# One attention loop of a twelve-stage kernel: maxima over one and two PSUM banks in turn, half sums by a product with a 0/1 matrix, value products in two bursts

## Chip, cores and metric

One core of a Trainium2 chip. The metric is the device time of one execution of the whole program in microseconds (us), the median of the runs shown.

## What is computed

The reference is a chain of four layers, each half a mixture of experts, an attention, half a mixture again, on x of shape (2, 1024, 128) in float32. The change lies in the attention of the first layer. With 16 heads of 8 channels, two batches and 1024 tokens it is a full softmax attention:

```
qp = (q @ wq.T + bq) * dh ** (-0.5); kp = k @ wk.T + bk; vp = v @ wv.T + bv
s = jnp.einsum('bqhd,bkhd->bhqk', qh, kh)
a = jax.nn.softmax(s, axis=-1)
o = jnp.einsum('bhqk,bkhd->bqhd', a, vh).reshape(B, Lq, D)
return o @ w_out.T + b_out
```

(There is a small attention across the two batches beside it, done once ahead of the loop.)

## The kernel before

Everything is written out by hand: five engines, each with its own list of instructions, and semaphores between them. The class `Full` and its functions `full_sync`, `full_pool`, `full_tensor`, `full_scalar` and `full_vector` are the first attention. Loops over the 32 pairs of a head and a batch are called phases here; four phases make a `turn` (`SLOTS` = 4), the first and the last turn stand alone and the six between them are a hardware loop.

q and k are split into three bf16 parts each and stored to DRAM; for a phase SyncE loads them back into one of four slots of `stack`, 72 rows of products, so that one bf16 product of 128 columns of stationary against 512 of moving gives a tile of exact scores (`by_query`, L1734: queries on the partitions, and `by_key`, L1751: keys on the partitions).

The softmax needs the maximum of each query before the exponential. So a phase does two things at once, for different heads and batches:

- for the phase two ahead, the maxima: 16 products `by_query` (8 query tiles of two halves of 512 keys), each reduced by VectorE to one number a partition (`piece`, L1947) into `nm2`. Products go through a ring of three banks, 0 to 2 (`RING`, `item`): product number i may be made when VectorE has done with number i - 3 (`ring_free`). When the 16 are done, `both_halves` (L1955) joins the halves, TensorE transposes the 8 columns (`turn_max`, L1742, an item of the ring too), VectorE copies them out (`max_out`, L1964), GpSimd splits them into three bf16 parts (`max_parts`, L1661 to L1664) and SyncE writes them as three more rows into the slot (`max_rows`, L1606), in time for the `by_key` of the next phase, which then gives scores minus maximum.
- for its own head and batch, scores by key: eight times two products into two banks (3 and 4 or 5 and 6), the exponential by ScalarE over both (L1877) into `pT`, and value products.

The value products (`values`, L1766) are f32, with 9 stationary columns (8 channels and a column of ones, which gives the softmax's sum) and 512 moving columns. Four of them run side by side in four column tiles of the array, all into bank 7: two halves of the queries, times odd and even key tiles. There are four such bursts of four products in a phase (m = 0 to 3), after the key tiles 4, 6 and 7 and, for m = 3, in the second step of the next phase. Since they all accumulate, a bf16 product of zeros clears the bank first (L1761).

Then bank 7 is copied by ScalarE (`o_copy`, L1864), transposed back by TensorE in four transposes into bank 7 (`by_token`, L1774), and VectorE adds the odd and the even half (`sums`, L1970) and takes the reciprocal of the sums (L1974); GpSimd divides (`divide`, L1669).

The order on TensorE within a phase, for kt = 0 to 7: a `by_query`, the two products of `by_key(kt)`, a `by_query`; after kt = 1 `turn_max` and the last value burst of the phase before; after kt = 2 `by_token` of the phase before; after kt = 4, 6 and 7 a value burst. Ahead of the loop stand two rounds of 16 maxima alone (the prologue), and the last two phases have none.

Of the kernel before, what the change touches and what calls it, by code (L numbers as in the profile page):

```python
# [8 lines left out]
ALU = mybir.AluOpType  # L9
# [3 lines left out]
P = 128  # L13
D = 128
B = 2
# [1481 lines left out]
class Full:  # L1497
# [17 lines left out]
    RING, SLOTS, PHASES = 3, 4, HEADS * B  # L1515
    TURNS = PHASES // SLOTS
    MAXIMA = TB * QH
    STEP = MAXIMA + 1
    LOADS, MAX_LOADS = 2 * 3 + 1, 3

    def __init__(self, k, n, w):
# [22 lines left out]
        self.oT_used = k.sem(f"{n}_oT_used")  # L1544
# [12 lines left out]
        self.nm2 = nm2.rearrange("p (a t h) -> p a t h", a=2, h=self.QH)  # L1557
# [13 lines left out]
    def item(self, t, q, i, alone=False):  # L1571

        at = (4 if not alone else 0) if i is None else i + (i >= 4 and q != -2)
# [55 lines left out]
def full_pool(pool, k, s):  # L1631
# [41 lines left out]
    def turn(t, first=False, last=False):  # L1673
        for q in range(s.SLOTS):
            n = t * s.SLOTS + q
            begin = first and q == 0
            fixed_values(n, t * (s.SLOTS // B) + q // B, q % B, q % 2, first=first and q < 2)
            if not (last and q == s.SLOTS - 1):
                if q == 0 and not first:
                    pool.wait_ge(s.stacked[s.SLOTS - 1], t * lap)  # L1680
                if q:
                    pool.wait_ge(s.stacked[q - 1], t * lap + lap)
                max_parts(n + 1, s.item(t, q, None, last and q == s.SLOTS - 2)[0], (q + 1) % 2)
            if not begin:
                divide(n - 1, t * (s.SLOTS // B) + (q - 1) // B, (q - 1) % B)

    max_parts(0, s.item(None, -1, None)[0], 0)
# [9 lines left out]
def full_tensor(pe, k, s):  # L1697
# [28 lines left out]
    def by_query(t, q, i, slot, laps):  # L1726

        _, bank, free = s.item(t, q, i)
        qt, half = divmod(i, s.QH)
        if i == 0:  # L1730
# [3 lines left out]
        pe.matmul(k.ps[:, bank, :], s.stack[:, slot, 0, qt * P:(qt + 1) * P],  # L1734
                  s.stack[:, slot, 1, half * GW:(half + 1) * GW], start=True, stop=True).then_inc(s.ring_full, 1)

    def turn_max(t, q, n, alone=False):

        _, bank, free = s.item(t, q, None, alone)
        pe.wait_ge(s.negmax, n + 1)  # L1740
        pe.wait_ge(s.ring_free, free)
        pe.transpose(k.ps[0:TB, bank, 0:P], s.nm, k.ident[:, :]).then_inc(s.ring_full, 1)  # L1742
# [12 lines left out]
    def values(n, m, place, first=False):  # L1755

        if m == 0:
            pe.wait_ge(s.vg, n + 1)
            if not first:
                pe.wait_ge(s.oT_used, n)  # L1760
            pe.matmul(k.ps[:, 7, :], k.zeros[:, 0:P], k.zeros[:, :], start=True, stop=False, skip_group_check=True)  # L1761
        pe.wait_ge(s.probs, n * TB + (2 * m + 2))
        for h in range(s.QH):
            for odd in range(2):
                at = 32 * (2 * h + odd)
                ins = pe.matmul(k.ps[at:at + s.DH + 1, 7, :], s.vs[:, place, 2 * m + odd, :],  # L1766
                                s.pT[:, 2 * m + odd, h * GW:(h + 1) * GW], start=False, stop=(m == TB // 2 - 1),
                                tile_position=(0, at), skip_group_check=True)
        ins.then_inc(s.values, 1)

    def by_token(n):
        pe.wait_ge(s.o_out, n + 1)
        for j in range(GT):
            ins = pe.transpose(k.ps[:, 7, j * P:(j + 1) * P], s.o[:, j * P:(j + 1) * P], k.ident[:, :])  # L1774
        ins.then_inc(s.oT_mm, 1)

    def turn(t, first=False, last=False):
        for q in range(s.SLOTS):
            n = t * s.SLOTS + q
            begin = first and q == 0  # L1780
            more = not (last and q >= s.SLOTS - 2)
            for kt in range(TB):
                if more:
                    by_query(t, q, 2 * kt, (q + 2) % s.SLOTS, t + (1 if q >= 2 else 0))
                by_key(n, kt, q, t, begin)
                if more:
                    by_query(t, q, 2 * kt + 1, (q + 2) % s.SLOTS, t + (1 if q >= 2 else 0))
# [9 lines left out]
    for i in range(s.MAXIMA):  # L1797
        by_query(None, -2, i, 0, 0)
    for i in range(s.MAXIMA):
        by_query(None, -1, i, 1, 0)  # L1800
        if i == 3:
            turn_max(None, -1, 0)
# [3 lines left out]
    turn(s.TURNS - 1, last=True)  # L1806
    values(s.PHASES - 1, 3, 1)
# [23 lines left out]
def full_scalar(act, k, s):  # L1831
# [51 lines left out]
    o_copy(s.PHASES - 1)  # L1883
    for g in range(NG):
# [5 lines left out]
def full_vector(dve, st, k, s):  # L1890
# [51 lines left out]
    def piece(t, q, i, place):  # L1942

        number, bank, _ = s.item(t, q, i)
        qt, half = divmod(i, s.QH)
        dve.wait_ge(s.ring_full, number + 1)
        dve.tensor_reduce(s.nm2[:, place, qt, half:half + 1], k.ps[:, bank, :], AX.X, ALU.max, negate=True)\  # L1947
            .then_inc(s.ring_free, 1)

    def both_halves(done, turned, place):  # L1950
# [4 lines left out]
        dve.tensor_reduce(s.nm, s.nm2[:, place, :, :], AX.X, ALU.min).then_inc(s.negmax, 1)  # L1955

    def max_out(t, q, n, alone=False):

        number, bank, _ = s.item(t, q, None, alone)
        dve.wait_ge(s.ring_full, number + 1)  # L1960
# [3 lines left out]
        dve.tensor_copy(s.nmf[0:TB, :], k.ps[0:TB, bank, 0:P]).then_inc(s.ring_free, 1)  # L1964

    def sums(n, first=False):
        dve.wait_ge(s.oT_mm, n + 1)
        if not first:
            dve.wait_ge(s.normalized, n)
        dve.tensor_reduce(s.sums[:, :, :].rearrange("p (h j) e -> p j h e", h=s.QH),  # L1970
                          k.ps[:, 7, :].rearrange("p (j h o z) -> p j h z o", j=GT, h=s.QH, o=2)[:, :, :, 0:s.DH + 1, :],
                          AX.X, ALU.add).then_inc(s.oT_used, 1)
        dve.wait_ge(s.oT_used, n + 1)
        dve.reciprocal(s.rsum[:, :], s.sums[:, :, s.DH]).then_inc(s.divisor, 1)  # L1974

    def turn(t, first=False, last=False):
        for q in range(s.SLOTS):
# [3 lines left out]
            if not (last and q == s.SLOTS - 1):  # L1981
                start, _, _ = s.item(t, q, 0)

                both_halves(start, start - 12, (q + 1) % 2)
            for kt in range(TB):
                if kt == 3 and not begin:
                    sums(n - 1, first=first and q == 1)
                if more:
                    piece(t, q, 2 * kt, q % 2)
                    piece(t, q, 2 * kt + 1, q % 2)  # L1990
# [3 lines left out]
    for i in range(s.MAXIMA):  # L1994
        piece(None, -2, i, 0)
    both_halves(s.MAXIMA, None, 0)
    for i in range(s.MAXIMA):
        piece(None, -1, i, 1)
        if i == 3:
            max_out(None, -1, 0)  # L2000
# [4 lines left out]
    sums(s.PHASES - 1)  # L2005
# [43 lines left out]
def build(nc, ins, out, plan):  # L2049
    with ExitStack() as ctx:  # L2050
# [24 lines left out]
        A0.wg, A0.wl, A0.cols = k.sb("l0a_wg", [P, 4, P]), k.sb("l0a_wl", [P, 4, P]), k.sb("l0a_cols", [P, 10])  # L2075
        A0.block, A0.bo, A0.blo, A0.scaled = k.sb("l0a_block", [P, P]), k.sb("l0a_bo", [P, D]), k.sb("l0a_blo", [1, D]), k.sb("l0a_scaled", [P, 2])
# [31 lines left out]
        def loads():  # L2108
# [9 lines left out]
            for m, dst in (("wg", A0.wg), ("wl", A0.wl), ("cols", A0.cols), ("block", A0.block), ("blo", A0.blo)):  # L2118
# [134 lines left out]
def layout(a):  # L2253
# [73 lines left out]
    out["l0a_block"] = out["l3_block"]  # L2327
    out["l0a_bo"], out["l0a_blo"] = a["L0_attn_bg_out"][None], a["L0_attn_bl_out"][None]
# [23 lines left out]
```

## Time and profile before

| | us |
|---|---|
| median of 3 runs | 2480.91 (2479.04 to 2482.99) |
| profiled execution | 2483.68 |
| its span, first to last instruction | 2481.9 |
| mean granted TensorE clock | 0.941 |

How to read the profile: times are microseconds from the start of the span; PE is TensorE's products, PEld its weight loads, DVE VectorE, ACT ScalarE, POOL GpSimd, SP SyncE. A group of instructions is named by line, engine, operation, out<-in and count; behind it stand the idle time of the engine just before it and what ended that. An f32 product appears as two records (two passes). Products are pipelined: a 512-column bf16 product is shown with 0.38 us but the next one starts 0.215 us later, so busy time of PE runs over short gaps, and an idle time of PEld is no idle time of the array. A few product records are missing.

### The profile page before, as it was taken

To read this page: it belongs to the slowest core of one execution; us is meant where nothing else is said; L and a number is where in the kernel's file an instruction comes from. 1 tells how busy PE (TensorE), PEld (TensorE's weight loads), DVE (VectorE), ACT (ScalarE), POOL (GpSimd) and SP (SyncE) were. 2 spreads that over 40 slices of the span, in tenths; PEclk is the share of its full clock that TensorE was granted. 3 is DMA by queue.
4 is the path that set the end of the run, shared out by engine and by line. 5 is a ranking of instruction groups with operands and counts; after the bars stand their busy time and mean duration, and the time that the engine had idled before them with its cause. 6 is when DMAs were issued, how large, how long until landed. Compare 5 with 4: busy or idle time off the path is not lost.

```text
span 2481.9 us, 39071 instructions
## 1 busy us (share of the span) xinstructions
PE 2165.2 (87%) x13425; PEld 1352.2 (54%) x13466; DVE 1570.0 (63%) x4488; ACT 1034.4 (42%) x1761; POOL 155.9 (6%) x273
## 2 busy tenths in 40 slices
PE   4559999995699989898999887999999579998698
PEld 3413333334577755555555554677766357775476
DVE  7688989858543346666665665334446735687766
ACT  2116767672143434444444443433333233343133
POOL 5111111114000000000000000000000000000000
PEclk8669999997799999999999999999999789999899
DMA  5020000000000000000000000000010000000000
GB/s 211 1 74 27 26 25 25 25 11 1 1 1 1 1 1 1 1 0 0 0 0 0 0 1 1 1 1 1 3 52 1 0 1 1 1 1 1 1 1 18
DMA packets 20864, 32.05 MB, mean 13 GB/s; under 512 B 5657, under 2 KB 12194, under 8 KB 19970
## 3 DMA queue, kind: packets, MB, share of 16 engines
q1 hardware_dynamic: 20738, 30.40, 3.6%
q8 instruction: 76, 1.25, 0.2%
q14 instruction: 50, 0.41, 0.1%
HBM read 25.80 MB, written 4.19 MB: 12 GB/s over the span
## 4 chain that ended last, share of the span: by engine, by line
PE 62%; DVE 10%; issue 3%; ACT 3%; DVEq 0%; ACTq 0%; POOL 0%; POOLq 0%
PE ps L404 18%; PE ps L389 18%; PE ps L600 6%; PE ps L634 5%; PE ps L617 4%; PE ps L584 3%; DVE arena L796 1%; ACT arena L730 1%; DVE x L814 1%; PE ps L606 1%; PE ps L330 1%; PE ps L252 1%; PE ps L896 1%; DVE stat L129 1%; PE ps L1050 1%
## 5 line engine op out<-in xcount | busy, mean ns | idle before, releaser
L404 PEld LDWEIGHTS ps<-l_w,arena 128*128 128x128 f32 x4096 | 543.6, 194 | 262.1 <-issue 248.4
L404 PE MATMUL ps<-l_w,arena 128*128 128x128 f32 x4096 | 546.8, 277 | 12.7 <-DVE x L491 10.9
L389 PE MATMUL ps<-xnT,l_w 128*128 128x512 f32 x1024 | 536.4, 607 | 3.0 <-ACT xnT L260 3.0
L491 DVE SCALAR_TENSOR_TENSOR x<-ps,comb,x 128x128 f32<-128x128 f32 x768 | 216.2, 344 | 378.2 <-PE ps L404 376.4
L447 ACT ACTIVATE arena<-ps,l_b 128x512 f32<-128x512 f32 x384 | 263.7, 687 | 408.9 <-PE ps L389 408.7
L1947 DVE TENSOR_REDUCE arena<-ps 128x1 f32<-128x512 f32 x512 | 325.5, 684 | 38.0 <-PE ps L1734 35.9
L1877 ACT ACTIVATE arena<-ps 128x1024 f32<-128x1024 f32 x256 | 252.5, 1023 | 128.6 <-PE ps L1751 128.2
L730 ACT ACTIVATE arena<-ps,arena 128x128 f32<-128x128 f32 (+7 forms) x256 | 187.1, 744 | 168.8 <-DVE arena L796 168.8
L796 DVE TENSOR_REDUCE arena<-ps 128x1 f32<-128x128 f32 (+7 forms) x256 | 179.0, 751 | 98.6 <-PE ps L606 98.6
L1734 PE MATMUL ps<-arena 128*128 128x512 bf16 x480 | 174.9, 398 | 6.7 <-DMA arena<-s_parts_k 4.1
L600 PE MATMUL ps<-arena 64*128 64x512 f32 (+3 forms) x768 | 151.1, 512 | 19.7 <-ACT arena L730 18.2
L389 PEld LDWEIGHTS ps<-xnT,l_w 128*128 128x128 f32 x1024 | 159.0, 195 | 16.5 <-issue 11.8
L617 PE MATMUL ps<-ident,arena 128*128 128x128 f32 x1152 | 163.8, 278 | 4.6 <-ACT arena L738 3.8
L803 DVE COPY arena<-ps 128x512 f32<-128x512 f32 (+1 forms) x192 | 99.0, 550 | 101.5 <-PE ps L617 99.4
L617 PEld LDWEIGHTS ps<-ident,arena 128*128 128x128 f32 x1152 | 128.1, 141 | 51.9 <-issue 27.7
L1751 PE MATMUL ps<-arena 128*128 128x512 bf16 x503 | 151.0, 382 | 4.0 <-DVE arena L1947 2.5
L738 ACT ACTIVATE arena<-ps 128x512 f32<-128x512 f32 (+1 forms) x192 | 86.1, 489 | 153.7 <-PE ps L617 153.4
L483 DVE SCALAR_TENSOR_TENSOR x<-l_b,comb,x 128x128 f32<-128x128 f32 x512 | 145.8, 347 | 4.2
L1734 PEld LDWEIGHTS ps<-arena 128*128 128x128 bf16 x512 | 50.2, 98 | 168.3 <-DVE arena L1947 122.1
L447 ACT ACTIVATE arena<-ps 128x512 f32<-128x512 f32 x128 | 76.5, 597 | 148.0 <-PE ps L389 147.7
L634 PE MATMUL ps<-arena 128*64 128x256 f32 (+3 forms) x1152 | 134.9, 383 | 0.9 <-issue 0.9
L1766 PE MATMUL ps<-arena,xn 128*9 128x512 f32 x1024 | 133.9, 595 | 0.1
(318 smaller groups left out, 2057.3 us busy)
## 6 DMA issues: line engine op xcount, KB each, us to landing
arena<-s_parts_q SPq DMA_DIRECT2D x96, 48.0 KB
arena<-s_parts_k SPq DMA_DIRECT2D x96, 48.0 KB
l_w<-in_l_w SPq DMA_DIRECT2D x2, 2048.0 KB, 14.2
l_w<-in_l_w SPq DMA_DIRECT2D x4, 1024.0 KB, 12.6
s_parts_q<-arena SPq DMA_DIRECT2D x2, 768.0 KB, 4.2
s_parts_k<-arena SPq DMA_DIRECT2D x2, 768.0 KB, 4.9
arena<-arena SPq DMA_DIRECT2D x96, 2.0 KB
x<-in_x SPq DMA_DIRECT2D x4, 256.0 KB, 3.5
```

The source lines that it names most:

```text
L389: pe.matmul(k.ps[:, n % 2, :], w.w1[:, e, f * P:(f + 1) * P], k.xnT[:, g * GW:(g + 1) * GW], start=True, stop=True).then_inc(s.hidden_mm.s ...
L404: ins = pe.matmul(k.ps[:, 2 + e % 4, j * P:(j + 1) * P], w.h[:, n % 2, j * P:(j + 1) * P], w.w2[:, e, f, :], start=(f == 0 and j == 0), st ...
L447: act.activation(w.h[:, n % 2, :], k.ps[:, n % 2, :], s.func, **kw).then_inc(s.hidden.sem, 1)
L491: ins = dve.scalar_tensor_tensor(k.x[:, t, :], k.ps[:, 2 + e % 4, j * P:(j + 1) * P], k.comb[:, t, e:e + 1], k.x[:, t, :], ALU.mult, ALU.add)
L600: pe.matmul(k.ps[:, 2 * h + i + c // GW, 0:n], s.q[rows, b, qt * P:(qt + 1) * P], s.kT[rows, b, c:c + n], start=True, stop=c + n < width, ...
L617: ins = pe.transpose(k.ps[:, 4 + i, j * P:(j + 1) * P], s.p[:, 2 * (u % 2) + h, at + j * P:at + (j + 1) * P], k.ident[:, :])
L634: ins = pe.matmul(k.ps[64 * h:64 * h + 64, 6, at:hi], s.v[:, b * TB + kt, 64 * h:64 * h + 64], s.pT[:, h, kt, at:hi], start=(kt == 0), sto ...
L730: ins = act.activation(s.p[:, 2 * (u % 2) + h, at:at + width], src[:, at:at + width], ACT.Exp, bias=s.nm[:, u % 2, h, i:i + 1], accum_out= ...
L796: ins = dve.tensor_reduce(s.nm[:, u % 2, h, i:i + 1], src[:, at:at + width], AX.X, ALU.max, negate=True)
L1734: pe.matmul(k.ps[:, bank, :], s.stack[:, slot, 0, qt * P:(qt + 1) * P], s.stack[:, slot, 1, half * GW:(half + 1) * GW], start=True, stop=T ...
L1877: act.activation(s.pT[:, kt, :], k.ps[:, bank:bank + 2, :].rearrange("p a b -> p (a b)"), ACT.Exp)\
L1947: dve.tensor_reduce(s.nm2[:, place, qt, half:half + 1], k.ps[:, bank, :], AX.X, ALU.max, negate=True)\
```

## The change

- The maxima of a phase are made in 11 groups, six of one product (always bank 2) and five of two products (banks 0 and 1), in turn, with the transpose of the maxima (bank 0) as the fourth of 12 places. One reduce of VectorE covers a group. A group may be made when the group two places back has been reduced. The order on TensorE is a table, `GROUPS_AT[kt, place]`, place 0 ahead of `by_key(kt)`, place 1 behind it.
- The clearing product is done once, in the first phase; each column tile's first value product starts its sum itself (`start=(m == 0)`).
- Value products come in two bursts of two steps: m = 0 and 1 after kt = 6, m = 2 and 3 after kt = 1 of the next phase.
- Four f32 products with the columns of `o` as the stationary operand and a 0/1 matrix `sel` (128 x 18, loaded with the weights) as the moving one take the place of the four transposes; they add odd and even halves. ScalarE copies the 72 numbers a partition to `sums` after the fourth exponential of the next phase, and VectorE only takes the reciprocal, ahead of its groups of kt = 4.

```
-    RING, SLOTS, PHASES = 3, 4, HEADS * B
+    SLOTS, PHASES = 4, HEADS * B
+    TURNED = 3
+    GROUPS = [(0, 1), (1, 3), (3, 4), None, (4, 5), (5, 7), (7, 8), (8, 10), (10, 11), (11, 13), (13, 14), (14, 16)]
+    STEP = len(GROUPS)
+    GROUPS_AT = {(0, 0): 0, (0, 1): 1, (1, 0): 2, (2, 0): 4, (2, 1): 5, (3, 0): 6, (3, 1): 7, (4, 0): 8, (5, 0): 9,
+                 (6, 0): 10, (7, 1): 11}
...
+    def group(self, t, q, j, alone=False):
+
         if t is None:
-            number = at + (self.MAXIMA if q == -1 else 0)
-            return number, number % self.RING, number - self.RING + 1
-        place = self.STEP * q + at
-        number = t * (self.STEP * self.SLOTS) + (self.MAXIMA + self.STEP + place)
-
-        return number, place % self.RING, number - (1 if place < 2 else self.RING - 1)
+            number = j - (q == -2 and j > self.TURNED) + (q == -1) * (self.STEP - 1)
+            return number, number - (0 if q == -2 and j == self.TURNED + 1 else 1)
+        number = 2 * self.STEP - 1 + (t * self.SLOTS + q) * self.STEP + (0 if alone else j)
+        return number, number - (0 if alone else 1)
...
+    def maxima(t, q, j, slot, laps):
+
+        _, free = s.group(t, q, j)
+        if j == 0:
             pe.wait_ge(s.stacked[slot], laps * lap + 16 * s.LOADS)
         if not (t is None and free <= 0):
             pe.wait_ge(s.ring_free, free)
+        lo, hi = s.GROUPS[j]
+        for i in range(lo, hi):
+            qt, half = divmod(i, s.QH)
+            ins = pe.matmul(k.ps[:, 2 if hi - lo == 1 else i - lo, :], s.stack[:, slot, 0, qt * P:(qt + 1) * P],
+                            s.stack[:, slot, 1, half * GW:(half + 1) * GW], start=True, stop=True)
+        ins.then_inc(s.ring_full, 1)
...
         if m == 0:
             pe.wait_ge(s.vg, n + 1)
-            if not first:
-                pe.wait_ge(s.oT_used, n)
-            pe.matmul(k.ps[:, 7, :], k.zeros[:, 0:P], k.zeros[:, :], start=True, stop=False, skip_group_check=True)
+            if first:
+                pe.matmul(k.ps[:, 7, :], k.zeros[:, 0:P], k.zeros[:, :], start=True, stop=True)
+            else:
+                pe.wait_ge(s.sums_out, n)
...
-            ins = pe.transpose(k.ps[:, 7, j * P:(j + 1) * P], s.o[:, j * P:(j + 1) * P], k.ident[:, :])
+            ins = pe.matmul(k.ps[:, 7, j * 18:(j + 1) * 18], s.o[:, j * P:(j + 1) * P], w.sel[:, :],
+                            start=True, stop=True)
...
+                for place in range(2):
+                    if more and (kt, place) in s.GROUPS_AT:
+                        maxima(t, q, s.GROUPS_AT[kt, place], (q + 2) % s.SLOTS, t + (1 if q >= 2 else 0))
+                    if place == 0:
+                        by_key(n, kt, q, t, begin)
                 if kt == 1 and not (last and q == s.SLOTS - 1):
                     turn_max(t, q, n + 1, alone=not more)
                 if kt == 1 and not begin:
+                    values(n - 1, 2, (q - 1) % 2)
                     values(n - 1, 3, (q - 1) % 2)
                 if kt == 2 and not begin:
                     by_token(n - 1)
-                if kt in (4, 6, 7):
-                    values(n, (4, 6, 7).index(kt), q % 2, first=begin)
+                if kt == 6:
+                    values(n, 0, q % 2, first=begin)
+                    values(n, 1, q % 2)
...
+    def sums(n, first=False):
+        act.wait_ge(s.oT_mm, n + 1)
+        if not first:
+            act.wait_ge(s.normalized, n)
+        act.activation(s.sums[:, :, :].rearrange("p (h j) e -> p j h e", h=s.QH),
+                       k.ps[:, 7, 0:18 * GT].rearrange("p (j h e) -> p j h e", h=s.QH, e=s.DH + 1), ACT.Copy)\
+            .then_inc(s.sums_out, 1)
...
+    def maxima(t, q, j, place):
+
+        lo, hi = s.GROUPS[j]
+        dve.wait_ge(s.ring_full, s.group(t, q, j)[0] + 1)
+        dve.tensor_reduce(s.nm2[:, place, lo:hi], k.ps[:, 2:3, :] if hi - lo == 1 else k.ps[:, 0:2, :],
+                          AX.X, ALU.max, negate=True).then_inc(s.ring_free, 1)
```

## Rows read from the trace of the kernel before

**Rows 1.** The page: span, and busy time, share and instructions of each engine.
```profile
span 2481.9 us, 39071 instructions
PE 2165.2 (87%) x13425; PEld 1352.2 (54%) x13466; DVE 1570.0 (63%) x4488; ACT 1034.4 (42%) x1761; POOL 155.9 (6%) x273
```

**Rows 2.** Windows, steady loop: length, busy PE PEld DVE ACT POOL, PEclk, DMA, GB/s.
```profile
300.00:420.00 120.00, 118.95 (x684) 38.12 (x696) 107.62 (x199) 83.94 (x90) 22.07 (x60) 1.00 0.08 26
```

**Rows 3.** Waits, 303 to 400 us: waiting <- releaser: us, times, longest.
```profile
PEld ps L1734 <- DVE arena L1947: 31.2, 41, 0.9
ACT arena L1877 <- PE ps L1751: 27.1, 40, 1.1
DVE arena L1947 <- PE ps L1734: 8.8, 30, 0.4
```

**Rows 4.** Line L1955 (once in each phase), same stretch: ns min/median/max, first and last start.
```profile
L1955 DVE TENSOR_REDUCE arena<-arena x8: 169/170/171, 315.0 to 399.9; 128x8 f32<-128x16 f32 x8
```

**Rows 5.** Groups of instructions, same stretch: count, busy us, mean ns, idle before.
```profile
L1947 DVE TENSOR_REDUCE arena<-ps 128x1 f32<-128x512 f32 x128 | 81.6, 685 | 9.2 <-PE ps L1734 8.8 <-remote 0.4
L1877 ACT ACTIVATE arena<-ps 128x1024 f32<-128x1024 f32 x64 | 63.1, 1023 | 27.1 <-PE ps L1751 27.1
...
L1970 DVE TENSOR_REDUCE arena<-ps 128x72 f32<-128x144 f32 x8 | 2.4, 297 | 0.0
```

**Rows 6.** Timeline, a phase's first part: start us, us, instruction, count, idle before.
```profile
400.24 0.59 PE L1751 MATMUL ps<-arena 128*128 128x512 bf16 x2
...
401.10 0.59 PE L1751 MATMUL ps<-arena 128*128 128x512 bf16 x2
...
401.83 0.27 PE L1742 MATMUL ps<-ident,arena 128*8 128x128 f32 x1
...
402.03 1.04 PE L1766 MATMUL ps<-arena,xn 128*9 128x512 f32 x8
...
403.01 0.39 PE L1734 MATMUL ps<-arena 128*128 128x512 bf16 x1
...
403.15 0.60 ACT L1864 ACTIVATE xn<-ps 128x512 f32<-128x512 f32 x1 [0.26 <-PE ps L1766]
...
403.44 0.69 DVE L1947 TENSOR_REDUCE arena<-ps 128x1 f32<-128x512 f32 x1 [0.28 <-PE ps L1734]
```

**Rows 7.** Timeline, the next 2.5 us: the transposes, a reduce and its follower.
```profile
403.89 0.60 PE L1774 MATMUL ps<-ident,xn 128*128 128x128 f32 x4
...
405.15 0.67 DVE L1947 TENSOR_REDUCE arena<-ps 128x1 f32<-128x512 f32 x1
...
405.87 0.39 PE L1734 MATMUL ps<-arena 128*128 128x512 bf16 x1
```

**Rows 8.** Timeline in a mixture: f32 products, 128x128 stationary, 8 columns.
```profile
674.68 3.27 PE L330 MATMUL ps<-l_gate,xnT 128*128 128x8 f32 x28
```

**Rows 9.** Timeline, second round of the prologue and start of phase 0.
```profile
157.87 2.00 PE L1734 MATMUL ps<-arena 128*128 128x512 bf16 x4 [2.59 <-DMA arena<-s_parts_k]
...
165.20 2.07 SPq L1606 DMA_DIRECT2D arena<-arena  x3
...
168.48 1.03 PE L1751 MATMUL ps<-arena 128*128 128x512 bf16 x2
```

**Rows 10.** Timeline: by_key starts of phases 30 and 31, first transpose after the loop.
```profile
533.59 1.04 PE L1751 MATMUL ps<-arena 128*128 128x512 bf16 x4
...
542.95 1.04 PE L1751 MATMUL ps<-arena 128*128 128x512 bf16 x4
...
556.00 1.35 PE L1813 MATMUL ps<-ident,acc 128*128 128x128 f32 x6 [1.08 <-POOL acc L1669]
```

**Rows 11.** Windows of later stages, columns as in Rows 2.
```profile
900.00:960.00 60.00, 48.40 (x319) 29.95 (x318) 32.57 (x75) 27.09 (x70) 0.53 (x2) 0.93 0.00 1
960.00:1240.00 280.00, 252.22 (x1882) 161.00 (x1882) 176.54 (x364) 136.42 (x342) 2.79 (x10) 1.00 0.00 0
1240.00:1560.00 320.00, 276.21 (x2047) 176.13 (x2044) 197.22 (x443) 147.67 (x361) 2.49 (x9) 0.98 0.00 0
```

More of the change, by code:

```diff
@@ L1569, in __init__, with start @@
         self.v = k.xnT.rearrange("p (t d) -> p t d", d=P)
-    def item(self, t, q, i, alone=False):
-        at = (4 if not alone else 0) if i is None else i + (i >= 4 and q != -2)
+    def group(self, t, q, j, alone=False):
         if t is None:
-            number = at + (self.MAXIMA if q == -1 else 0)
-            return number, number % self.RING, number - self.RING + 1
-        place = self.STEP * q + at
-        number = t * (self.STEP * self.SLOTS) + (self.MAXIMA + self.STEP + place)
-        return number, place % self.RING, number - (1 if place < 2 else self.RING - 1)
+            number = j - (q == -2 and j > self.TURNED) + (q == -1) * (self.STEP - 1)
+            return number, number - (0 if q == -2 and j == self.TURNED + 1 else 1)
+        number = 2 * self.STEP - 1 + (t * self.SLOTS + q) * self.STEP + (0 if alone else j)
+        return number, number - (0 if alone else 1)
+    def start(self, t, q):
+        return 2 * self.STEP - 1 + (t * self.SLOTS + q) * self.STEP
 def full_sync(sp, k, s):
@@ L1682, in turn @@
                     pool.wait_ge(s.stacked[q - 1], t * lap + lap)
-                max_parts(n + 1, s.item(t, q, None, last and q == s.SLOTS - 2)[0], (q + 1) % 2)
+                max_parts(n + 1, s.group(t, q, s.TURNED, last and q == s.SLOTS - 2)[0], (q + 1) % 2)
             if not begin:
                 divide(n - 1, t * (s.SLOTS // B) + (q - 1) // B, (q - 1) % B)
-    max_parts(0, s.item(None, -1, None)[0], 0)
+    max_parts(0, s.group(None, -1, s.TURNED)[0], 0)
     turn(0, first=True)
@@ L1733, in by_query @@
             pe.wait_ge(s.ring_free, free)
-        pe.matmul(k.ps[:, bank, :], s.stack[:, slot, 0, qt * P:(qt + 1) * P],
-                  s.stack[:, slot, 1, half * GW:(half + 1) * GW], start=True, stop=True).then_inc(s.ring_full, 1)
+        lo, hi = s.GROUPS[j]
[4 more added lines that the diff above has]
+        ins.then_inc(s.ring_full, 1)
     def turn_max(t, q, n, alone=False):
-        _, bank, free = s.item(t, q, None, alone)
+        _, free = s.group(t, q, s.TURNED, alone)
         pe.wait_ge(s.negmax, n + 1)
         pe.wait_ge(s.ring_free, free)
-        pe.transpose(k.ps[0:TB, bank, 0:P], s.nm, k.ident[:, :]).then_inc(s.ring_full, 1)
+        pe.transpose(k.ps[0:TB, 0, 0:P], s.nm, k.ident[:, :]).then_inc(s.ring_full, 1)
     def by_key(n, kt, slot, laps, first):
@@ L1766, in values @@
                 ins = pe.matmul(k.ps[at:at + s.DH + 1, 7, :], s.vs[:, place, 2 * m + odd, :],
-                                s.pT[:, 2 * m + odd, h * GW:(h + 1) * GW], start=False, stop=(m == TB // 2 - 1),
+                                s.pT[:, 2 * m + odd, h * GW:(h + 1) * GW], start=(m == 0), stop=(m == TB // 2 - 1),
                                 tile_position=(0, at), skip_group_check=True)
@@ L1793, in turn @@
                     by_token(n - 1)
-                if kt in (4, 6, 7):
-                    values(n, (4, 6, 7).index(kt), q % 2, first=begin)
[L1797 to L1802, printed above, removed]
+                if kt == 6:
+                    values(n, 0, q % 2, first=begin)
+                    values(n, 1, q % 2)
+    for q in (-2, -1):
+        for j in range(s.STEP):
+            if j != s.TURNED:
+                maxima(None, q, j, q + 2, 0)
+            elif q == -1:
+                turn_max(None, q, 0)
     turn(0, first=True)
@@ L1806, in full_tensor @@
     turn(s.TURNS - 1, last=True)
+    values(s.PHASES - 1, 2, 1)
     values(s.PHASES - 1, 3, 1)
@@ L1872, in turn @@
                     o_copy(n - 1, first=first and q == 1)
+                if kt == 4 and not begin:
+                    sums(n - 1, first=first and q == 1)
                 act.wait_ge(s.scores, n * TB + (kt + 1))
@@ L1883, in full_scalar @@
     o_copy(s.PHASES - 1)
+    sums(s.PHASES - 1)
     for g in range(NG):
@@ L1954, in both_halves @@
             dve.wait_ge(s.ring_full, turned)
-        dve.tensor_reduce(s.nm, s.nm2[:, place, :, :], AX.X, ALU.min).then_inc(s.negmax, 1)
+        dve.tensor_reduce(s.nm, s.nm2[:, place, :].rearrange("p (t h) -> p t h", h=s.QH), AX.X, ALU.min).then_inc(s.negmax, 1)
     def max_out(t, q, n, alone=False):
-        number, bank, _ = s.item(t, q, None, alone)
-        dve.wait_ge(s.ring_full, number + 1)
+        dve.wait_ge(s.ring_full, s.group(t, q, s.TURNED, alone)[0] + 1)
         if t is not None:
@@ L1963, in max_out, with divisors @@
             dve.wait_ge(s.negmax, n + 1)
-        dve.tensor_copy(s.nmf[0:TB, :], k.ps[0:TB, bank, 0:P]).then_inc(s.ring_free, 1)
-    def sums(n, first=False):
-        dve.wait_ge(s.oT_mm, n + 1)
+        dve.tensor_copy(s.nmf[0:TB, :], k.ps[0:TB, 0, 0:P]).then_inc(s.ring_free, 1)
+    def divisors(n, first=False):
+        dve.wait_ge(s.sums_out, n + 1)
         if not first:
             dve.wait_ge(s.normalized, n)
[L1970 to L1973, printed above, removed]
         dve.reciprocal(s.rsum[:, :], s.sums[:, :, s.DH]).then_inc(s.divisor, 1)
@@ L1981, in turn @@
             if not (last and q == s.SLOTS - 1):
-                start, _, _ = s.item(t, q, 0)
-                both_halves(start, start - 12, (q + 1) % 2)
+                both_halves(s.start(t, q), s.start(t, q) - (s.STEP - s.TURNED - 1), (q + 1) % 2)
             for kt in range(TB):
[L1986 to L1990, printed above, removed]
+                if kt == 4 and not begin:
+                    divisors(n - 1, first=first and q == 1)
+                for place in range(2):
+                    if more and (kt, place) in s.GROUPS_AT:
+                        maxima(t, q, s.GROUPS_AT[kt, place], q % 2)
                 if kt == 1 and not (last and q == s.SLOTS - 1):
                     max_out(t, q, n + 1, alone=not more)
[L1994 to L2000, printed above, removed]
+    for q in (-2, -1):
+        for j in range(s.STEP):
+            if j != s.TURNED:
+                maxima(None, q, j, q + 2)
+            elif q == -1:
+                max_out(None, q, 0)
+        if q == -2:
+            both_halves(s.STEP - 1, None, 0)
     turn(0, first=True)
@@ L2004, in full_vector @@
     turn(s.TURNS - 1, last=True)
-    sums(s.PHASES - 1)
+    divisors(s.PHASES - 1)
     dve.wait_ge(s.biased, 1)
@@ L2117, in loads @@
                 yield F0, dst[:], row.broadcast_to([P, row.shape[1]])
-            for m, dst in (("wg", A0.wg), ("wl", A0.wl), ("cols", A0.cols), ("block", A0.block), ("blo", A0.blo)):
+            for m, dst in (("wg", A0.wg), ("wl", A0.wl), ("cols", A0.cols), ("block", A0.block), ("blo", A0.blo),
+                           ("sel", A0.sel)):
                 yield A0, dst[:], ins[f"l0a_{m}"]
@@ L2327, in layout @@
     out["l0a_block"] = out["l3_block"]
+    columns = 9 * (np.arange(4) // 2)[:, None] + np.arange(9)[None, :]
+    out["l0a_sel"] = np.zeros((4, 32, 18), np.float32)
+    for quarter in range(4):
+        out["l0a_sel"][quarter, np.arange(9), columns[quarter]] = 1.0
+    out["l0a_sel"] = out["l0a_sel"].reshape(P, 18)
     out["l0a_bo"], out["l0a_blo"] = a["L0_attn_bg_out"][None], a["L0_attn_bl_out"][None]
```

22 lines of the change are left out of this document (3 added, 19 removed).

## The prediction

> **What bounds the kernel now.** I read the page's totals first [rows 1]: TensorE is busy 87% of 2481.9 us, VectorE 63%, but such shares mix stages. The change touches one stage, the first attention (147 to 556 us), whose body is 32 phases, one for each head and batch. In a steady stretch of it [rows 2] TensorE is busy 118.95 of 120.00 us at full granted clock (1.00, the 2.4 GHz level), VectorE 107.62, ScalarE 83.94. A phase lasts (399.9 - 315.0)/7 = 12.13 us [rows 4]. So VectorE has 1.25 us of slack in a phase and ScalarE 3.65; TensorE has almost none. The waits [rows 3] say the same: the 31.2 us of "PEld waits for DVE" are weight loads waiting while the array still streams the products before them; the array itself hardly stops.
>
> TensorE's phase adds up [rows 6, 7]. A bf16 product of 512 columns takes 0.215 (four from 400.24 to 401.10). The 32 of a phase are 6.9, the clearing product 0.22, the maximum's transpose 0.20 (401.83 to 402.03), the four transposes of o 0.44 ((0.60 - 0.27)/3 = 0.11 each), and four bursts of value products 0.98 each (402.03 to 403.01) with some 0.1 to change over before each: 4.3. Sum 12.06 of 12.13. It is bound by its own work.
>
> **Why it never stops now** is the ring. Three banks, one product each; a product needs the reduce three items back. One reduce is 0.69 (next start 0.60 later), so while VectorE works at one bank two more are full or filling. Two latencies matter below: the start of a product to the start of a waiting reduce, 0.43 after a stop (403.01 to 403.44), 0.42 in a stream; the end of a reduce to the product that waits for it, 405.87 - (405.15 + 0.67) = 0.05 [rows 6, 7].
>
> **Part 1, maxima over one and two banks in turn.** Six reduces of 512 stay, five of 1024 replace ten. From 144 elements in 0.297 and 512 in 0.685 [rows 5] an element costs 1.05 ns, so a reduce over two banks takes 0.685 + 0.54 = 1.22; the other bound is two back to back, 0.60 + 0.60 = 1.20. I take 1.22. VectorE saves some 5 x 0.07 = 0.35 in a phase, on an engine with slack: worth nothing. What counts is the ring. A group now needs the group two back, and the two-bank groups all use banks 0 and 1 (so does the transpose, bank 0). From the first product of a pair to the first of the next use of its banks: 0.215 + 0.42 + 1.22 + 0.05 = 1.91 us. What TensorE has to do in between is only the pair, a single and one by_key: 5 x 0.215 = 1.08. Where nothing else stands between, TensorE must stop for 0.8 us. Before, three items back left 1.15 to cover (0.43 + 0.67 + 0.05) and there was nearly always that much.
>
> **Part 2, zero product gone, two bursts.** The clearing product: -0.22. A double burst: the four column tiles run together, groups of four passes 0.44 apart (1.04 - 0.60), the last to the next product 0.54 (0.98 - 0.44), so 3 x 0.44 + 0.54 = 1.86, against 2 x 0.98, and one change over less: -0.2 each, -0.4 a phase. Bounds: 1.75 to 1.96.
>
> **Part 3, half sums by a product with a 0/1 matrix.** Four transposes (0.44) become four f32 products with 128x128 stationary o and 18 columns. The trace has this shape with 8 columns: passes 0.112 apart ((3.27 - 0.26)/27) [rows 8], two for each product, so 8 x 0.112 = 0.89; bounds 0.44 and 0.95. +0.45. The Trainium skill's "TensorEngine Tiling (Array Packing)", Instruction Overhead, puts a short product at some 60 cycles whatever its columns; an estimate from that page would be 0.2 for the eight, but this case's 0.112 a pass speaks against it, and it leaves out the f32 weight load. VectorE's sum of 0.30 goes; ScalarE gets a copy of 72 elements, 0.2 to 0.6, inside its 3.65 of slack. VectorE's reciprocal waits for that copy now, with the next reduces queued behind it: the copy stands after the fourth exponential, near 9.5 us of the new phase, and VectorE comes to the reciprocal at 10.0. No loss. TensorE's next value products want the copy at 11.7. No loss.
>
> If nothing stopped, TensorE would need 12.13 - 0.22 - 0.4 + 0.45 - 0.1 (its small gaps now) = 11.86 a phase.
>
> **The phase laid out by hand.** Zero is the first product of a phase; g0 to g11 are the groups (g3 the transpose, T), K0 to K7 the by_key pairs, D a two-bank reduce. A product after a stop takes 0.23, then 0.215.
> - g0 at 0, K0 to 0.65. g1 needs the D of the last g11, whose second product started at -0.22: D from 0.20 to 1.42. g1 at 1.47: **0.8 stopped**.
> - VectorE: both_halves, then g0 from 1.60 to 2.28, g1 from 2.20 to 3.41. g2 needs g0: 2.33, TensorE was free at 1.92: **0.4 stopped**. K1 to 2.99. T needs g1: 3.46: **0.5 stopped**.
> - Double burst from 3.66; g4 at 5.52, K2, g5 at 6.18, free at 6.61. o's copy (0.60 [rows 6]) runs from 5.66 to 6.26, in time. Selection product to 7.51. g6, K3, g7 at 8.16 (it needs g5's D, which ends at 8.04: just in time). g8 needs g6: 8.70, **0.1 stopped**, K4 to 9.36.
> - g9 needs g7's D, 8.80 to 10.02: 10.07, **0.7 stopped**. K5, g10 near 10.95, K6 to 11.6, double burst from 11.7 to 13.55, K7, g11 from 13.98, next phase at 14.42.
>
> Check: 11.86 of work and 2.5 of stops, 14.4. VectorE idles too (some 4 us): neither engine is the bound, the handshake is. The maximum rows don't matter: their copy now ends near 4.2 of a phase, GpSimd is busy 22.07/10 = 2.2 in a whole phase [rows 2], and from the issue of their DMAs to the product that waits for them it took 3.3 in the prologue (165.20 to 168.48) [rows 9], so they are there by 9.7 of 14.4. The bound of the costs moves little, because the chain is mostly reduces and latencies: with D 1.20 and a burst of 1.75, 14.1; with 1.23 and 1.96, 14.7.
>
> **The sum.** Phases 1 to 29 have maxima and values: 29 x (14.42 - 12.13) = +66.4. Phase 0 has no values of a phase before: +0.5. The prologue (maxima alone): now three banks take 3 x 0.60 = 1.80; at the lower clock level, where it mostly runs (two by_key products take 1.03 there, 0.43 and 0.60 [rows 9]), a pair and a single will take 1.22 + 0.05 + 0.43 + 0.60 + 0.04 = 2.34, +0.5 for three banks. The second round starts with a DMA at 157.87 either way, and TensorE's by_key waits at 168.48 for the maximum rows whose DMAs were issued from 165.20 [rows 9], behind the loads of the slots, which hides a part: I take +2, between 0 and +4. Phases 30 and 31 have no maxima and now take 9.36 and, with the tail, 13.05 (533.59, 542.95, 556.00) [rows 10]. A double burst there stops ScalarE longer than its two pairs of banks cover; laid out likewise they come to 10.9 and 11.3, and the end (one more value step, 0.89 for 0.44, the copy on ScalarE) to 1.4 more: +5, between 0 and +8. Sum +74. The profiled execution was 2481.9 of span and 2483.68 in all, 2.8 above the median of 2480.91; the difference is added to the median: 2555.
>
> **Rivals.**
> - (A) Forecast: the two-deep ring stops TensorE, 14.4 a phase: 2555.
> - (B) Faster. The stops don't come, because TensorE's other work covers the two-bank reduce; the phase is 11.86, -0.27 x 29 = -8, with prologue and tail about even: 2473. It decides at 1.91 us from pair to pair: were a two-bank reduce 0.4 us, it would be covered by 1.08 of work. No row of this trace reads 1024 elements that fast; ScalarE, too, takes 1.02 for 1024 [rows 5]. For it speaks only that TensorE's work shrinks. With the 60 cycles of the Trainium skill's "TensorEngine Tiling (Array Packing)" it would be 0.7 a phase less still, an estimate of 2453, and A only 0.07 a phase less, since g7 would then wait for g5.
> - (C) The stops also drop the granted clock. The loop would have TensorE busy some 88% of the time. The nearest rows [rows 11]: 252.22 of 280 us at clock 1.00, 276.21 of 320 at 0.98, 48.40 of 60 at 0.93. At 0.93 the loop's 450 us would lose up to 7%, +30: 2585. The Trainium skill's "TensorE: Matmul & The Clock Gate", A second HAM failure mode, names this pattern (cycling through PSUM banks, short idles between groups) as one that makes the clock swing; the rows above, with like idle shares and a full clock, speak against it here.
> - (D) The change doesn't cost what its edits say: the flags of the value products alter values, not time, and nothing leaves the loop; I give no separate price.
>
> **How the numbers follow.** A 0.82, C 0.10, B 0.06, something in between near no change 0.02. The predicted time is A's. Its own range is 2544 to 2568 from the bounds above (29 x 0.3 = 9, prologue and tail 3 to 5); to hold 8 in 10 it is widened for C and for one stop that I laid out wrongly (0.4 x 29 = 12 to 20 either way): 2535 to 2585. A measurement of this kernel tells about 0.2% from no change. Faster 0.06, same 0.02, slower 0.92.
>
> **What would show it.** Right: steady phases of 14.4; TensorE products waiting for the two-bank reduce with real gaps in the products (not only in weight loads) ahead of g1, g2, T and g9; VectorE busy near 10 us of a phase with more idle than before; a two-bank reduce of 1.22; a double burst of 1.86; 0.112 between passes of the selection product; clock 1.00. Wrong if the phase is under 12.1 (then the ring covers more than I read from the waits), if the two-bank reduce is clearly under 1.2, or if the clock row of the loop falls under 0.98.

## The result and the profile after

The changed kernel takes 2555.89 us (2552.35 to 2557.82, 4 runs) against 2480.16 (2479.04 to 2482.99): ratio 1.030, 95% interval 1.028 to 1.032. It is slower by 76 us; 2555 was forecast, in 2535 to 2585. The profiled execution is the fastest of the four, 2552.35 with a span of 2550.6.

The page of after, totals, and then the window of the steady loop (length, busy PE, PEld, DVE, ACT, POOL, granted clock, DMA, GB/s), which answer to [rows 1] and [rows 2]:

```profile
span 2550.6 us, 38921 instructions
PE 2171.6 (85%) x13516; PEld 1360.7 (53%) x13563; DVE 1548.7 (61%) x4296; ACT 1044.3 (41%) x1793; POOL 155.6 (6%) x273
```

```profile
300.00:420.00 120.00, 103.32 (x605) 36.24 (x617) 84.21 (x118) 72.91 (x83) 19.26 (x52) 1.00 0.07 22
```

VectorE has less work in all (1548.7 for 1570.0). But in the loop TensorE is busy 103.32 of 120 for 118.95, and VectorE 84.21 for 107.62, at a full granted clock: both stand more often. The waits of 313 to 400 us tell on whom (waiting <- releaser: us, times, longest):

```profile
PEld ps L1737 <- DVE arena L1966: 23.9, 31, 1.2
DVE arena L1966 <- PE ps L1737: 20.3, 16, 2.1
...
PE ps L1737 <- DVE arena L1966: 10.2, 19, 0.9
...
PE ps L1746 <- DVE arena L1966: 1.8, 6, 0.3
```

The new lines are the last two: the products of the maxima and their transpose (PE, not only PEld) wait for VectorE's reduce, 12.0 us in six phases, and VectorE waits 20.3 for TensorE, where it waited 8.8 in eight phases before [rows 3]. Each waits for the other in turn.

Length of a phase, by the line that joins the halves (L1955 before, L1974 after; ns min/median/max, then first and last start), starts of phases 1 and 30, of before and of after:

```profile
L1955 DVE TENSOR_REDUCE arena<-arena x30: 169/170/171, 181.3 to 533.4; 128x8 f32<-128x16 f32 x30
```

```profile
L1974 DVE TENSOR_REDUCE arena<-arena x30: 169/170/171, 182.4 to 600.8; 128x8 f32<-128x16 f32 x30
```

352.1/29 = 12.14 and 418.4/29 = 14.43 us: +66.3 of the difference lie in these 29 phases.

One phase of after in the timeline (start, length, instruction, count, idle before and its releaser), to be held against the layout of the prediction with its zero at 397.47:

```profile
397.04 0.81 PE L1737 MATMUL ps<-arena 128*128 128x512 bf16 x3
...
397.67 1.23 DVE L1966 TENSOR_REDUCE arena<-ps 128x2 f32<-128x1024 f32 x1 [2.06 <-PE ps L1737]
397.69 0.59 PE L1755 MATMUL ps<-arena 128*128 128x512 bf16 x2
...
398.95 0.61 PE L1737 MATMUL ps<-arena 128*128 128x512 bf16 x2 [0.67 <-DVE arena L1966]
399.03 0.17 DVE L1974 TENSOR_REDUCE arena<-arena 128x8 f32<-128x16 f32 x1
399.24 2.42 DVE L1966 TENSOR_REDUCE arena<-ps 128x1 f32<-128x512 f32 x3
...
399.99 0.39 PE L1737 MATMUL ps<-arena 128*128 128x512 bf16 x1 [0.43 <-DVE arena L1966]
...
401.12 0.27 PE L1746 MATMUL ps<-ident,arena 128*8 128x128 f32 x1 [0.31 <-DVE arena L1966]
...
401.32 1.90 PE L1771 MATMUL ps<-arena,xn 128*9 128x512 f32 x16
...
403.15 0.39 PE L1737 MATMUL ps<-arena 128*128 128x512 bf16 x1
...
403.58 0.69 DVE L1966 TENSOR_REDUCE arena<-ps 128x1 f32<-128x512 f32 x1 [1.70 <-PE ps L1737]
...
404.25 0.96 PE L1779 MATMUL ps<-l0a_sel,xn 128*128 128x18 f32 x8
...
405.06 0.38 PE L1737 MATMUL ps<-arena 128*128 128x512 bf16 x1
...
406.82 0.23 ACT L1879 ACTIVATE arena<-ps 128x72 f32<-128x72 f32 x1
...
407.51 0.19 DVE L1988 RECIPROCAL arena<-arena 128x8 f32<-128x8 f32 x1
...
407.65 0.60 PE L1737 MATMUL ps<-arena 128*128 128x512 bf16 x2 [0.51 <-DVE arena L1966]
```

Read the four bracketed PE lines; they are g1, g2, T and g9. The first line is the pair g11 (397.04, 397.25) and then g0 (397.47). g1 (398.95) starts 0.05 after the end of g11's two-bank reduce (397.67 + 1.23), and 1.91 after the first product of that pair. The idle times shown count from a product's modelled end; counted from when the next could have started (its start + 0.215) TensorE is stopped 0.84 ahead of g1 (by_key's second product at 397.69 + 0.21, next possible 398.11), 0.59 ahead of g2, 0.47 ahead of T (by_key's second product at 400.43, next possible 400.65) and 0.67 ahead of g9. On the other side VectorE stands 2.06 us until g11 comes behind a double burst and 1.70 until g4 comes behind the other. The double burst takes 403.15 - 401.32 = 1.83.

### The profile page after: what moved, and what is told of

Its sections match the earlier page's. It is cut to its first block, busy times and chain, and to the rows that moved or that the text cites. A ratio compares the mean times of both kernels' runs of the same rounds, so it can differ in the third digit from the quotient of the medians.

```text
span 2550.6 us, 38921 instructions
## 1 busy us (share of the span) xinstructions
PE 2171.6 (85%) x13516; PEld 1360.7 (53%) x13563; DVE 1548.7 (61%) x4296; ACT 1044.3 (41%) x1793; POOL 155.6 (6%) x273
## 4 chain that ended last, share of the span: by engine, by line
PE 60%; DVE 9%; issue 3%; ACT 3%; DVEq 0%; ACTq 0%; POOL 0%; POOLq 0%
PE ps L404 18%; PE ps L389 17%; PE ps L600 6%; PE ps L634 5%; PE ps L617 4%; PE ps L584 3%; ACT arena L730 1%; DVE arena L796 1%; DVE x L814 1%; PE ps L606 1%; PE ps L330 1%; PE ps L252 1%; PE ps L896 1%; DVE stat L129 1%; PE ps L1050 1%
## 5 line engine op out<-in xcount | busy, mean ns | idle before, releaser
L1966 DVE TENSOR_REDUCE arena<-ps 128x1 f32<-128x512 f32 (+1 forms) x352 | 315.3, 926 | 128.1 <-PE ps L1737 111.2
L1896 ACT ACTIVATE arena<-ps 128x1024 f32<-128x1024 f32 x256 | 258.1, 1024 | 156.5 <-PE ps L1755 151.9
L1737 PE MATMUL ps<-arena 128*128 128x512 bf16 x495 | 165.5, 400 | 57.8 <-DVE arena L1966 55.5
L1755 PE MATMUL ps<-arena 128*128 128x512 bf16 x482 | 146.5, 382 | 6.1 <-ACT arena L1896 3.2
L1737 PEld LDWEIGHTS ps<-arena 128*128 128x128 bf16 x512 | 44.5, 103 | 183.9 <-DVE arena L1966 133.9
L1771 PE MATMUL ps<-arena,xn 128*9 128x512 f32 x1024 | 122.1, 593 | 1.2
```

The lines of the kernel that those rows point to most:

```text
L1737: ins = pe.matmul(k.ps[:, 2 if hi - lo == 1 else i - lo, :], s.stack[:, slot, 0, qt * P:(qt + 1) * P], s.stack[:, slot, 1, half * GW:(half ...
L1966: dve.tensor_reduce(s.nm2[:, place, lo:hi], k.ps[:, 2:3, :] if hi - lo == 1 else k.ps[:, 0:2, :], AX.X, ALU.max, negate=True).then_inc(s.r ...
```

## Experiments

Two explanations stand against that of the ring. **Ring**: two groups, with banks 0 and 1 in use 1.9 us at a time, stop TensorE. **Bursts**: the double bursts starve VectorE, and that is what is paid. **Select**: the product with the 0/1 matrix takes more of TensorE than was reckoned. The phase lengths below all come from the line that joins the halves, as above, phases 1 to 29, and the table gathers them behind the last experiment. Ratios are to the kernel before in the same round of runs.

**Part 1 alone**: groups and ring of the changed kernel, with four bursts, clearing product, transposes and VectorE's sums as before. The edit is shown against the changed kernel:

```
+            pe.matmul(k.ps[:, 7, :], k.zeros[:, 0:P], k.zeros[:, :], start=True, stop=False, skip_group_check=True)
...
-            ins = pe.matmul(k.ps[:, 7, j * 18:(j + 1) * 18], s.o[:, j * P:(j + 1) * P], w.sel[:, :],
-                            start=True, stop=True)
+            ins = pe.transpose(k.ps[:, 7, j * P:(j + 1) * P], s.o[:, j * P:(j + 1) * P], k.ident[:, :])
...
-                    values(n - 1, 2, (q - 1) % 2)
...
-                if kt == 6:
-                    values(n, 0, q % 2, first=begin)
-                    values(n, 1, q % 2)
+                if kt in (4, 6, 7):
+                    values(n, (4, 6, 7).index(kt), q % 2, first=begin)
```

> The kernel before with part 1 alone: groups of one and two banks in turn; value products in four bursts, the clearing product, the transposes and VectorE's sums as before. Theory Ring (the two-group ring stops TensorE because one use of banks 0 and 1 takes 1.9 us and too little stands between two uses): laid out by hand, TensorE stops ahead of g2 (0.25), T (0.5), g7 (0.4) and g8 (0.7), phase 13.8, and with the prologue about 2534. Rival Bursts (the double bursts starve VectorE and that is what is paid): phase near 12.1, about 2482 with the prologue. Rival Select (the longer product of the half sums): 2480.

Measured 2530.19, ratio 1.019 (1.018 to 1.021), phase 13.86. The groups alone cost 1.72 us a phase, without any double burst or selection product. Bursts and Select as sole causes fall. TensorE's stops in the timeline are where they were laid out: 0.25 ahead of g2 (405.53), 0.58 ahead of T (406.76), 0.39 ahead of g7 (410.51) and 0.60 ahead of g8 (411.56), for 0.25, 0.5, 0.4 and 0.7.

**Parts 2 and 3**, on the ring of three single banks (the kernel before with both edits below):

> The kernel before with parts 2 and 3 and its ring of three single banks. Ring: most stops go; but a double burst of 1.86 us is longer than the banks that are full when it starts, so VectorE runs dry and TensorE then waits for it, laid out 13.0 a phase, about 2510. Bursts: all of the loss stays, 14.4 a phase, 2552. Select alone: 12.2 a phase, 2484.

Measured 2518.86, ratio 1.015 (1.013 to 1.016), phase 13.30. Of the 2.29 that the whole change costs, 1.13 go with the groups; 1.16 stays without them. So parts 2 and 3 together have a price of their own, more than I laid out (13.0). The timeline shows where VectorE runs dry: it stands 1.14 and 0.90 behind the two bursts (the first began at 394.88). Three banks are 1.9 us of reduces at best (0.69 + 2 x 0.60, an estimate from [rows 6] and the 0.60 from start to start), and one of them is already in work.

```profile
396.71 0.39 PE L1734 MATMUL ps<-arena 128*128 128x512 bf16 x1
...
397.14 1.34 DVE L1963 TENSOR_REDUCE arena<-ps 128x1 f32<-128x512 f32 x2 [1.14 <-PE ps L1734]
...
402.85 1.90 PE L1767 MATMUL ps<-arena,xn 128*9 128x512 f32 x16
...
405.11 1.34 DVE L1963 TENSOR_REDUCE arena<-ps 128x1 f32<-128x512 f32 x2 [0.90 <-PE ps L1734]
```

**Part 2 alone**, on the kernel before (no clearing product, two double bursts):

```
...
+                    values(n - 1, 2, (q - 1) % 2)
                     values(n - 1, 3, (q - 1) % 2)
...
-                if kt in (4, 6, 7):
-                    values(n, (4, 6, 7).index(kt), q % 2, first=begin)
+                if kt == 6:
+                    values(n, 0, q % 2, first=begin)
+                    values(n, 1, q % 2)
```

> The kernel before with part 2 alone: no clearing product, two double bursts, ring of three single banks, transposes, VectorE's sums. TensorE's work would be 11.5 a phase, but VectorE needs 10.9 and cannot be fed during 1.86 us with at most three banks full. Laid out: 12.7 a phase, about 2501. If the ring covers the burst: 11.5, 2461.

Measured 2503.56, ratio 1.009 (1.007 to 1.011), phase 12.77. By the estimates of the prediction TensorE saves 0.6 us of work, and the phase grows by 0.6.

**Part 3 alone**, on the kernel before (selection product, ScalarE's copy, reciprocal alone on VectorE):

```
-            ins = pe.transpose(k.ps[:, 7, j * P:(j + 1) * P], s.o[:, j * P:(j + 1) * P], k.ident[:, :])
+            ins = pe.matmul(k.ps[:, 7, j * 18:(j + 1) * 18], s.o[:, j * P:(j + 1) * P], w.sel[:, :],
+                            start=True, stop=True)
...
+                if kt == 4 and not begin:
+                    sums(n - 1, first=first and q == 1)
```

> The kernel before with part 3 alone: selection product on TensorE, copy on ScalarE, reciprocal alone on VectorE. Ring and Bursts: TensorE is the bound and gets 0.81 (measured in the trace of after) for 0.44, so +0.37 in each of 31 phases, +11, 2491. Select as the main cause: over +40, 2520 or more.

Measured 2506.57, ratio 1.010 (1.008 to 1.011), phase 12.89. That is 15.6 us above what was expected: 0.75 a phase, twice the 0.37. Its timeline has the other half:

```profile
404.96 0.38 PE L1734 MATMUL ps<-arena 128*128 128x512 bf16 x1
405.22 0.23 ACT L1871 ACTIVATE arena<-ps 128x72 f32<-128x72 f32 x1
...
405.59 0.38 PE L1761 MATMUL ps<-zeros 128*128 128x512 bf16 x1 [0.25 <-ACT arena L1871]
```

The clearing product may not touch bank 7 before the copy is out, and the copy is queued behind an exponential. TensorE, free at 405.18, starts at 405.59. To test it, the copy one exponential earlier:

```
-                if kt == 4 and not begin:
+                if kt == 3 and not begin:
                     sums(n - 1, first=first and q == 1)
```

> The kernel with part 3 alone, and ScalarE's copy of the sums one exponential earlier (ahead of that of kt 3). In the run with part 3 alone the clearing product stood 0.41 us (405.18 to 405.59) until that copy, made behind the exponential of kt 3, had ended. If this wait is the second half of what part 3 cost, it goes: 12.5 a phase for 12.89, 2494. If the selection product itself costs more than its 0.37 (slower passes, or VectorE's waits), the time stays at 2506.

Measured 2493.26, ratio 1.005 (1.003 to 1.006), phase 12.48. The wait was worth 0.41 of the 0.75; the 0.34 left agrees with the longer product (0.81 for 0.44).

**The length of the two-bank reduce**, in the changed kernel. This kernel leaves half the keys of the two-bank groups out of the maxima:

```
-        dve.tensor_reduce(s.nm2[:, place, lo:hi], k.ps[:, 2:3, :] if hi - lo == 1 else k.ps[:, 0:2, :],
+        dve.tensor_reduce(s.nm2[:, place, lo:hi], k.ps[:, 2:3, :] if hi - lo == 1 else k.ps[:, 0:2, 0:GW // 2],
```

> The changed kernel, but the reduce over two banks reads only the first 256 of the 512 columns in each, so that its maxima cover half the keys of these groups; every instruction, wait and place stays, only the reduce takes some 0.69 for 1.22. Ring: the round trip of banks 0 and 1 falls from 1.91 to 1.38 and most stops with it, laid out 12.8 a phase, about 2508. Bursts or Select: the chain doesn't go through the reduce, so no more than 0.2 a phase, 2548 or above.

Measured 2508.91, ratio to before 1.011 (1.009 to 1.013), phase 12.91. Only the reduce got shorter: 0.69 on the mean of 34, for 1.22. That is five times 0.53 us = 2.65 of VectorE's work in a phase, on an engine that stood idle over 4 us of it, and the phase lost 1.52. So the end of that reduce is on the chain.

**What stands between two uses of banks 0 and 1**, in the changed kernel:

```
+                if kt == 1 and not begin:
+                    values(n - 1, 3, (q - 1) % 2)
                 if kt == 1 and not (last and q == s.SLOTS - 1):
                     turn_max(t, q, n + 1, alone=not more)
-                if kt == 1 and not begin:
-                    values(n - 1, 2, (q - 1) % 2)
-                    values(n - 1, 3, (q - 1) % 2)
...
-                if kt == 6:
-                    values(n, 0, q % 2, first=begin)
-                    values(n, 1, q % 2)
+                if kt in (4, 6, 7):
+                    values(n, (4, 6, 7).index(kt), q % 2, first=begin)
...
-                if kt == 4 and not begin:
+                if kt == 3 and not begin:
                     sums(n - 1, first=first and q == 1)
```

> The changed kernel with its groups, its ring and its selection product, but each value burst alone and put between two uses of banks 0 and 1: after kt 4, 6 and 7, and in kt 1 ahead of the transpose T instead of behind it; ScalarE's copy of the sums stands one exponential earlier, so that the burst after kt 4 finds it done. Ring: 1.91 us are now covered nearly everywhere, TensorE is back at its own work, 12.2 plus one stop of 0.25 ahead of g2, 12.4 a phase, about 2492. Bursts: also better, since the bursts are single, but by its price from ring3_rest only. If two groups are too few whatever stands between: over 13.5 a phase, 2525.

Measured 2503.93, ratio 1.008 (1.007 to 1.010), phase 12.66. The window of its steady loop, columns as above:

```profile
300.00:420.00 120.00, 118.92 (x695) 39.01 (x698) 97.86 (x134) 84.89 (x96) 21.53 (x58) 1.00 0.09 26
```

TensorE is busy 118.92 of 120 again. The groups and the two-deep ring are the same, TensorE has even more work (two more changes over), and the phase is 1.77 us shorter. The bursts are single here as well, so their own price has to be kept apart: parts 2 and 3 without the groups cost 1.16, less than the 1.77; and part 1 alone, with single bursts too but none ahead of T, stood at 13.86 (it also has VectorE's sums in the way of its reduces, and no run parts the two). The timeline shows the places directly:

```profile
400.40 0.59 PE L1755 MATMUL ps<-arena 128*128 128x512 bf16 x2
400.83 1.07 PE L1737 MATMUL ps<-arena 128*128 128x512 bf16 x3
...
402.27 1.04 PE L1771 MATMUL ps<-arena,xn 128*9 128x512 f32 x8
...
403.24 0.27 PE L1746 MATMUL ps<-ident,arena 128*8 128x128 f32 x1
...
407.27 1.05 PE L1771 MATMUL ps<-arena,xn 128*9 128x512 f32 x8
...
408.25 0.60 PE L1737 MATMUL ps<-arena 128*128 128x512 bf16 x2
```

g1 (400.83) follows by_key at once, and T (403.24) and g9 (408.25) follow a burst at once: the stops of 0.84, 0.47 and 0.67 are gone, each where a burst now stands between the two uses of banks 0 and 1. What is left is 0.26 ahead of g2, as laid out, and 0.2 ahead of g7 and g8 (405.92 and 406.53), which was not: most of the 0.25 by which the phase is longer than the 12.4 I had laid out. The earlier copy is not what made the phase shorter, since nothing waited for the copy in the changed kernel.

**TensorE's own work as the bound of the kernel before**, its clearing product left out:

```
             if not first:
                 pe.wait_ge(s.oT_used, n)
-            pe.matmul(k.ps[:, 7, :], k.zeros[:, 0:P], k.zeros[:, :], start=True, stop=False, skip_group_check=True)
+            else:
+                pe.matmul(k.ps[:, 7, :], k.zeros[:, 0:P], k.zeros[:, :], start=True, stop=True)
...
-                                s.pT[:, 2 * m + odd, h * GW:(h + 1) * GW], start=False, stop=(m == TB // 2 - 1),
+                                s.pT[:, 2 * m + odd, h * GW:(h + 1) * GW], start=(m == 0), stop=(m == TB // 2 - 1),
```

> The kernel before without the clearing product (done once in the first phase; the first value product of each column tile starts its sum), nothing else. If TensorE's own work is the bound of the kernel before: -0.22 in each of 31 phases, -7, about 2473.5 (ratio 0.997). If VectorE or the ring is a second bound close by: no change, 2480.

Measured 2476.68 (7 runs) against 2482.84 (11 runs), ratio 0.9974 (0.9963 to 0.9985), phase 11.93: -0.21 a phase, the length of the product. So this kernel is faster than both, by 0.26% of the kernel before.

| kernel | phase, us | time, us | ratio to before |
|---|---|---|---|
| before | 12.14 | 2480.16 | |
| no clearing product | 11.93 | 2476.68 | 0.997 |
| part 3 alone, copy earlier | 12.48 | 2493.26 | 1.005 |
| changed, bursts between the pairs | 12.66 | 2503.93 | 1.008 |
| part 2 alone | 12.77 | 2503.56 | 1.009 |
| part 3 alone | 12.89 | 2506.57 | 1.010 |
| changed, reduce over half the columns | 12.91 | 2508.91 | 1.011 |
| parts 2 and 3 | 13.30 | 2518.86 | 1.015 |
| part 1 alone | 13.86 | 2530.19 | 1.019 |
| changed | 14.43 | 2555.89 | 1.030 |

The three parts alone cost 1.72, 0.63 and 0.75, which would be 3.1; together they cost 2.29. Of the difference, 0.41 is the wait of the clearing product for ScalarE's copy, which the changed kernel doesn't have. That the other 0.4 lies hidden in the stops, where one engine waits for the other anyway, is an argument and not shown.

## Why the prediction was right, point by point

- **What bounds the kernel before** (TensorE's own work): held. Taking 0.22 of work away gave 0.21.
- **The two-bank reduce, 1.22**: the trace of after has 1.223 on the mean of 31 (group below). That VectorE's saving is worth nothing was not tried by itself; part 1 alone has it and is 1.72 a phase slower.

```profile
L1966 DVE TENSOR_REDUCE arena<-ps 128x2 f32<-128x1024 f32 x31 | 37.9, 1223 | 14.2 <-PE ps L1737 13.4
```

- **The round trip of 1.91 against 1.08 of cover**: held. The timeline has 1.91 (397.04 to 398.95), and the last two experiments on the changed kernel show it from two sides, a shorter reduce and a longer cover.
- **The layout**: 14.42 for a mean of 14.43; the phase shown lasts 14.50 (397.47 to 411.97). The stops are where I put them, but not quite of that size: ahead of g1 0.84 (0.8), g2 0.59 (0.4), T 0.47 (0.5), g8 0.16 (0.1), g9 0.67 (0.7). Their sum is 2.7 and not 2.5. both_halves ran 0.13 behind the two-bank reduce it waits for, and the next reduce began only at its end (399.24), 0.17 later than laid out; g2 waits for that. The close agreement of the whole phase owes something to misses of opposite sign: the stops came out 0.2 longer, while the selection product took 405.06 - 404.25 = 0.81, not 0.89, and each double burst 1.83, not 1.86.
- **The selection product**: the row of 8 columns carried over to 18. By the estimate from the Trainium skill's "TensorEngine Tiling (Array Packing)", Instruction Overhead, it would have been 0.2 for the eight passes; measured were 0.81.
- **ScalarE's copy, "no loss"**: right for the changed kernel (copy ended at 407.05, reciprocal began at 407.51 behind a reduce), but only because its next value products come after kt = 6 (409.26). With part 3 alone, whose clearing product comes after kt = 4, the same copy stopped TensorE 0.41 us a phase. The step was argued from the slack of ScalarE; what decided was what the copy is queued behind.
- **The bursts**: costed as a gain of 0.4 for TensorE, with VectorE's hunger seen only inside the layout. Alone they cost 0.6 a phase. This didn't hurt the forecast, since the layout had it in, but the -0.4 in the list of parts gives a wrong picture of it.
- **The sum**: phases 1 to 29 +66.3 (forecast +66.4). Phase 0: 13.5 for 12.9, +0.6 (+0.5). The prologue, from its first reduce to the start of phase 0, 25.3 for 21.6 (146.76 to 168.40 before, 143.68 to 168.93 after): +3.6, not +2. A pair and a single took 2.35 (149.10 to 151.45), as forecast (2.34), but less of it was hidden behind DMAs than I took: the second round now starts at 156.16 behind a reduce, where before it started at 157.87 behind a DMA [rows 9]. From phase 30 to the first transpose behind the loop (626.36 - 600.81 against 556.00 - 533.44) +3.0, not +5. In all +73.5 for +74: that it comes so close is in part luck, since prologue and end missed by 1.6 and 2.0 in opposite directions. The rest of the program, untouched, was 3.1 us earlier at the loop and 1.7 shorter behind it in this execution, which is why the spans differ by 68.7 only; the medians differ by 75.7. The 2.2 between 73.5 and 75.7 are not placed.
- **The clock (C)**: fell. The granted clock was 1.00 from 200 to 620 us, with some 2.7 us of stops in a phase of 14.4. The Trainium skill's "TensorE: Matmul & The Clock Gate", A second HAM failure mode, tells of another kernel that cycled through PSUM banks with short idles, and whose clock swung; in this trace, with stops of 0.1 to 0.8 us, it didn't.
- **B** (the stops don't come) fell with the first bracketed line of the timeline.

Not tried: a fourth bank for the ring (all eight are taken), and a ring of two pairs.

## What to carry to other kernels

Count the depth of a ring in groups that can be in flight, not in banks: three banks as a single and a pair hold only two groups, and the time from a pair's first product to the next use of its banks (products, latency, reduce, release) has to be covered by other work between just these two places. Where neither engine is the bound by its busy time, lay one period out by hand from the rows' starts and ends, in the order written in the code; adding up the work of the parts gave neither the sign nor the size here. And before fusing bursts to save changes of tile shape, see whether the engine fed by the other products has that long a store.

## What the hardware showed that was not expected

The first of eight f32 passes with 18 columns was followed by the second at once, so eight took 0.81 and not 8 x 0.112. With 8 columns [rows 8] and with 18 a pass takes the same 0.11 us, so it isn't the columns that are paid for: such a product has two passes and costs 0.2 us, where an f32 transpose of 128 columns is one record and takes 0.11 [rows 7]. What sets the 0.11 was not tried.
